# A GRU image scan on one core: the columns' second sum, t2, as a matmul with the unit matrix in 99 of 512 steps

## The reference, cut to what matters

```
def step(h, xg):
    hg = h @ W_hh.T + b_hh
    xr, xz, xn = jnp.split(xg, 3, axis=-1)
    hr, hz, hn = jnp.split(hg, 3, axis=-1)
    r = jax.nn.sigmoid(xr + hr)
    z = jax.nn.sigmoid(xz + hz)
    n = jnp.tanh(xn + r * hn)
    h_new = (1.0 - z) * n + z * h
    return (h_new, h_new)
...
return (right + down + left + up) / 4.0
```

## Time and profile before

| | |
|---|---|
| median of three runs | 2451.59 us |
| the profiled execution's own time | 2460.0 us |
| its span, first to last instruction | 2458.2 us |
| busy in the span: TensorE, VectorE, ScalarE, GpSimd | 88%, 81%, 65%, 62% |
| granted TensorE clock, mean over the span | 0.983 |

### The profile page before, as it was taken

The page is one execution under the profiler, slowest core; times in us unless marked ns, Lnnn a source line. Parts: engine busy times, 40 slices in busy tenths (PEclk is TensorE's granted clock), DMA queues, the critical chain, the costliest instruction groups (busy, mean ns, idle before and its releaser), DMA issues.

```text
span 2458.2 us, 81224 instructions
## 1 busy us (share of the span) xinstructions
PE 2158.5 (88%) x32176; PEld 1391.8 (57%) x32176; DVE 1997.6 (81%) x4912; ACT 1587.1 (65%) x3423; POOL 1534.5 (62%) x2119
## 2 busy tenths in 40 slices
PE   0679999899979999999979999999989999999993
PEld 0345555566646666566646666565646666665551
DVE  7309999877769999888869999888867887888883
ACT  0126666677757888677757788677757888887610
POOL 2007777667766777667766677667766777777710
PEclk9999999999989999999989999999999999999997
DMA  9993332245689998589999998589988666663379
GB/s 348 287 241 99 98 98 79 81 145 174 199 253 278 263 251 217 150 217 278 268 287 281 250 249 220 149 222 270 275 249 230 148 156 150 159 151 96 91 264 365
DMA packets 325720, 509.27 MB, mean 207 GB/s; under 512 B 24928, under 2 KB 140000, under 8 KB 325344
## 3 DMA queue, kind: packets, MB, share of 16 engines
q1 hardware_dynamic: 307296, 478.23, 70.0%
q10 hardware_dynamic: 18048, 25.85, 3.0%
HBM read 352.98 MB, written 151.01 MB: 205 GB/s over the span
## 4 chain that ended last, share of the span: by engine, by line
DVE 33%; PE 30%; ACT 17%; issue 7%; DMA 7%; POOL 3%; SPq 2%; ACTq 0%; DVEq 0%; POOLq 0%
PE bank L889 19%; DVE r L1033 11%; DVE r L1038 10%; ACT r L691 7%; DMA work<-x 5%; DVE h L1052 5%; ACT z L695 5%; DVE bank L1043 2%; ACT bank L699 2%; PE bank L869 2%; ACT work L686 2%; PE bank L871 2%; DVE bn L1025 2%; PE bank L890 1%; POOL hsum L567 1%
## 5 line engine op out<-in xcount | busy, mean ns | idle before, releaser
L889 PE MATMUL bank<-h,wh 64*64 64x256 f32 x6144 | 1493.4, 386 | 112.9 <-DVE h L1052 94.1
L869 PE MATMUL bank<-seq,wx 64*64 64x256 f32 x6144 | 1545.6, 384 | 31.3 <-DMA seq<-seq_next 22.6
L871 PE MATMUL bank<-seq,wx 64*64 64x256 f32 x6144 | 1547.4, 385 | 2.2 <-issue 2.2
L890 PE MATMUL bank<-h,wh 64*64 64x256 f32 x6144 | 1495.1, 387 | 0.0
L575 POOL TENSOR_TENSOR v<-z,h 128x256 f32<-128x256 f32 x1024 | 746.1, 729 | 617.8 <-ACT z L695 591.9
L889 PEld LDWEIGHTS bank<-h,wh 64*64 64x64 f32 x6144 | 713.1, 133 | 576.4 <-DVE h L1052 414.0
L869 PEld LDWEIGHTS bank<-seq,wx 64*64 64x64 f32 x6144 | 756.4, 133 | 194.4 <-DVE r L1038 94.4
L583 POOL TENSOR_TENSOR hsum<-hsum,h 128x256 f32<-128x256 f32 x1024 | 750.7, 733 | 129.3 <-DVE h L1052 106.9
L871 PEld LDWEIGHTS bank<-seq,wx 64*64 64x64 f32 x6144 | 754.5, 133 | 35.4 <-issue 4.2
L1033 DVE SCALAR_TENSOR_TENSOR r<-bank,bhh,r 128x256 f32<-128x256 f32 x1024 | 490.9, 479 | 277.3 <-ACT r L691 246.0
L890 PEld LDWEIGHTS bank<-h,wh 64*64 64x64 f32 x6144 | 704.1, 133 | 0.8
(11 more groups left out here) (94 smaller groups left out, 2441.4 us busy)
## 6 DMA issues: line engine op xcount, KB each, us to landing
work<-x SPq DMA_DIRECT2D x384, 384.0 KB, 6.2
work<-x SPq DMA_DIRECT2D x144, 512.0 KB, 6.0
out<-work SPq DMA_DIRECT2D x192, 384.0 KB, 4.9
work<-x SPq DMA_DIRECT2D x288, 128.0 KB, 6.0
work<-x SPq DMA_DIRECT2D x32, 768.0 KB, 6.5
seq_next<-work SPq DMA_DIRECT2D x48, 512.0 KB, 6.4
work<-hsum_last SPq DMA_DIRECT2D x48, 512.0 KB, 7.4
seq<-x SPq DMA_DIRECT2D x16, 512.0 KB, 7.0
```

The costliest lines, as they stand in the source:

```text
L869: pe.matmul(as_pair(ps[LOW, :], c), wx[HIGH, gate, :], px[HIGH], start=start, stop=False, skip_group_check=True)
L871: return pe.matmul(as_pair(ps[HIGH, :], c), wx[LOW, gate, :], px[LOW], start=start, stop=False, skip_group_check=True)
L889: pe.matmul(ps[LOW, 0:N2], wh[LOW, gate, :], state[LOW], start=start, stop=True, skip_group_check=True)
L890: return pe.matmul(ps[HIGH, 0:N2], wh[HIGH, gate, :], state[HIGH], start=start, stop=True, skip_group_check=True)
```

## The change

In the two stretches named above (the first pair's steps 0 to 69, and the fourth pair's steps 99 to 127: `t2_on_pe`), chain 1 is handled in another way:

- xn goes to bank 4 beside hn in place of bank 3; n and u go to the second half of bank 5, beside z, in place of bank 4.
- VectorE no longer makes t2 of chain 1. In its place TensorE multiplies t1 with the unit matrix and adds the product to xn in bank 4 (`add_t1`, two matmuls on the straight quarters), between x_n0 and x_z0. It waits for t1 and releases n.
- ScalarE's n of chain 1 reads bank 4 and writes bank 5; before, it read SBUF and wrote bank 4.
- x_z1 moves behind h_r1, and waits for h of chain 1. x_n1 now waits for n of the step before; x_r1 waits for r of the step before in place of t2.

```
+        def t2_on_pe(g, t):
+            return (g == 0 and t < PROJECT_FROM - 1) or (g + 1 == PAIRS and t > max(last_unit_at))
+        def xn_ps(g, t, c):
+            return hn_ps[1][:, N2:2 * N2] if c == 1 and t2_on_pe(g, t) else rx_ps[c][:, N2:2 * N2]
+        def n_ps(g, t, c):
+            return z_ps[1][:, N2:2 * N2] if c == 1 and t2_on_pe(g, t) else hn_ps[c][:, 0:N2]
+        def u_ps(g, t, c):
+            return z_ps[1][:, N2:2 * N2] if c == 1 and t2_on_pe(g, t) else hn_ps[c][:, N2:2 * N2]
...
-                act.activation(hn_ps[c][:, 0:N2], r[:, c, :], ACT.Tanh, bias=bih[:, 2:3]).then_inc(n_ready[c], 1)
+                before = xn_ps(g, t, c) if c == 1 and t2_on_pe(g, t) else r[:, c, :]
+                act.activation(n_ps(g, t, c), before, ACT.Tanh, bias=bih[:, 2:3]).then_inc(n_ready[c], 1)
...
+                if c == 1 and t > 0 and t2_on_pe(g, t - 1):
+                    pe.wait_ge(h_ready[1], state_before(g, t))
                 x_part(z_ps[c][:, 0:N2], 1, c, t, True).then_inc(x_z_ready[c], 1)
...
+                beside_state = c == 1 and t2_on_pe(g, t)
+                if beside_state and t > 0:
+                    if t2_on_pe(g, t - 1):
+                        pe.wait_ge(n_ready[1], T * g + t)
+                    else:
+                        pe.wait_ge(h_ready[1], state_before(g, t))
+                x_part(xn_ps(g, t, c), 2, c, t, beside_state).then_inc(x_rn_ready[c], 1)
...
+            def add_t1(g, t):
+                sums = xn_ps(g, t, 1)
+                pe.wait_ge(t1_ready[1], T * g + t + 1)
+                pe.matmul(sums[LOW], ident[LOW, :], r[LOW, 1, :], start=False, stop=True, skip_group_check=True)
+                pe.matmul(sums[HIGH], ident[HIGH, :], r[HIGH, 1, :], start=False, stop=True,
+                          skip_group_check=True).then_inc(t2_ready[1], 1)
...
-                    x_z(g, t, 1)
+                    if not t2_on_pe(g, t):
+                        x_z(g, t, 1)
 
                     h_r(g, t, 1)
+                    if t2_on_pe(g, t):
+                        x_z(g, t, 1)
...
+                    if t2_on_pe(g, t):
+                        add_t1(g, t)
                     if t + 1 < T:
                         x_z(g, t + 1, 0)
...
-                    make_t2(g, t, 1)
+                    if not t2_on_pe(g, t):
+                        make_t2(g, t, 1)
                     make_h(g, t, 0)
```

More of the change, by code:

```diff
@@ L880, in x_r @@
                 if T * g + t > 0:
-                    pe.wait_ge(t2_ready[c], T * g + t)
+                    pe.wait_ge(r_ready[1] if c == 1 and t > 0 and t2_on_pe(g, t - 1) else t2_ready[c], T * g + t)
                 x_part(rx_ps[c][:, 0:N2], 0, c, t, True)
             def x_n(g, t, c):
-                x_part(rx_ps[c][:, N2:2 * N2], 2, c, t, False).then_inc(x_rn_ready[c], 1)
+                beside_state = c == 1 and t2_on_pe(g, t)
[5 more added lines that the diff above has]
+                x_part(xn_ps(g, t, c), 2, c, t, beside_state).then_inc(x_rn_ready[c], 1)
             def h_part(ps, gate, t, c, start):
@@ L899, in h_n @@
             def h_n(g, t, c):
-                h_part(hn_ps[c], 2, t, c, True).then_inc(pre_n[c], 1)
+                h_part(hn_ps[c], 2, t, c, not (c == 1 and t2_on_pe(g, t))).then_inc(pre_n[c], 1)
+            def add_t1(g, t):
[4 more added lines that the diff above has]
+                          skip_group_check=True).then_inc(t2_ready[1], 1)
             def h_z(g, t, c):
@@ L1037, in make_t2 @@
                 dve.wait_ge(t1_ready[c], T * g + t + 1)
-                dve.tensor_tensor(r[:, c, :], rx_ps[c][:, N2:2 * N2], r[:, c, :], ALU.add).then_inc(t2_ready[c], 1)
+                dve.tensor_tensor(r[:, c, :], xn_ps(g, t, c), r[:, c, :], ALU.add).then_inc(t2_ready[c], 1)
             def make_u(g, t, c):
                 dve.wait_ge(n_ready[c], T * g + t + 1)
-                dve.scalar_tensor_tensor(out=hn_ps[c][:, N2:2 * N2], in0=z[:, c, :], scalar=1.0, in1=hn_ps[c][:, 0:N2],
+                dve.scalar_tensor_tensor(out=u_ps(g, t, c), in0=z[:, c, :], scalar=1.0, in1=n_ps(g, t, c),
                                          op0=ALU.subtract, op1=ALU.mult).then_inc(u_ready[c], 1)
@@ L1051, in make_h @@
                     dve.wait_ge(h_added[c], k - 1)
-                dve.tensor_tensor(h[:, c, t % 2, :], v[:, c, :], hn_ps[c][:, N2:2 * N2], ALU.subtract)\
+                dve.tensor_tensor(h[:, c, t % 2, :], v[:, c, :], u_ps(g, t, c), ALU.subtract)\
                    .then_inc(h_ready[c], 1)
```

## The result

The changed kernel takes 2446.32 us, median of 20 runs (2435.16 to 2450.19); the kernel before took 2455.64 on the same chip, median of 20 (2443.53 to 2466.44). The ratio is 0.9961 with a 95% interval of 0.9949 to 0.9973: 9.6 us faster, 6.6 to 12.5. The ratio is not the quotient of the two medians, and the medians can differ by a few us more or less; here they differ by 9.3 us. Two later measurements of the same program, beside the kernel before on two other occasions, gave 12.7 and 14.2 us (12.0 and 10.8 by the medians); all three, weighted by their intervals, give 11.2 us, with 2.3 either way. The forecast was a saving of 18.3 us.

What follows compares the result with a forecast made beforehand. A loop through several engines, with chain 1's t2 in it, was taken to bound the step; 13.0 us (first pair) plus 5.3 us (fourth) gave 18.3 us off 2451.59: 2433.3, say 2434 us, range 2429 to 2443.

Steps and rivals of the forecast that it cites:

- Loops A, B and C: Step loops: A through both chains without t2, 3.84 us; B chain 1's own, 3.85; C VectorE's order, first pair only, 3.85.
- Unknown (1): Link from t1 through TensorE's unit matmuls to n of chain 1: taken as 0.75 us, at best 0.69, at worst 1.18.
- Unknown (2): ScalarE's n of chain 1 from PSUM to PSUM: taken as 0.48 us, at most a tenth of a microsecond either way.
- The sum of 20.0 us by that rule: Whole saving if ScalarE's cheaper PSUM reads made n 43 ns shorter, leaving the 3.84 us loop to bind.
- Unknown (3): h_r1 on TensorE becoming a late starter: second pass 0.27 us behind the first, not 0.21, chain 1's loop then 3.90.
- rival 3: Unit matmuls take turns with x_z0 on TensorE: link 1.18 us, 24 us slower, 2475; chance 0.06.
- I put all of this at nothing: New waits of x_n1, x_r1 and x_z1 in TensorE's queue cost nothing; x_n1 has 0.06 us of room.
- Steps 64 to 69 ... I count them as the others: First pair's steps longer than 4.05 us, with u, t2, h in the same order, gain as much as plain steps.
- The fourth pair at 3.85 and 29 times 0.183: Fourth pair's 29 changed steps fall from 4.033 to 3.85 us each, saving 5.3 us.
- The other stretches step as before: Sign of being right: steps outside the two changed stretches keep their length.
- The end: Fourth pair's 5.3 us reach the program's end whole; the output stage begins and ends earlier by as much.
- rival 4: The program's end hides the fourth pair's saving: only 13.0 us remain, 2439; chance 0.25 together with another rival.

Runs made afterwards that it cites:

- no_t2: Kernel before with chain 1's t2 (and so xn in n) left out in the 99 steps, computing something else: 2438.14 us, ratio 0.9919.
- slow_first: Kernel before with one more VectorE operation between u of chain 0 and t2 of chain 1 in the first pair's steps 0 to 69: 2478.84 us, ratio 1.0091.
- long_link: Changed kernel with the two unit matmuls issued twice, the first time into a bank nobody reads: 2481.75 us, ratio 1.0088 against the kernel before.
- the six programs above: Six programs with TensorE code as before up to the fourth pair's changed steps; the steps the change leaves alone sum to 1289.3 us in their mean.
- slow_fourth: Kernel before with one more VectorE operation between u of chain 0 and t2 of chain 1 in the fourth pair's steps 99 to 127: 2463.4 us, ratio 1.0034.
- fourth_only: The change in the fourth pair's steps 99 to 127 alone, against the kernel before: 2452.81 us, ratio 0.9975.
- pad_after: Changed kernel with 158 small unneeded matmuls at the start of TensorE's program, against the kernel before: ratio 0.994, 14.7 us less.
- old_order: Changed kernel with x_z1 ahead of h_r1 again, keeping its new wait for h of chain 1: 2468.76 us in a single run, kernel before 2455.97.

## Why the prediction was right and where it was wrong

- **What bounds the step**: right. It is the loop h_r0, h_r1, r1, t1, u, h with t2 of chain 1 standing in it; without t2 the step is 3.850 (no_t2), with one more operation in that place it is longer by just that operation (slow_first).
- **Loops A, B and C at 3.84, 3.85, 3.85, taken as 3.86**: right, 3.863 measured (C not by itself, as said). Unknown (1), the link, is 0.75. Unknown (2): n from PSUM to PSUM is 0.45 us, 0.03 less than from SBUF. The rule of the Trainium skill (VectorE: DVE Perf Modes, section on the TRN2 errata) has 52 cycles for this difference, an estimate of 43 ns: the row goes the same way, with 0.03 of the 0.043 us. The sum of 20.0 us by that rule did not come. Unknown (3): the second pass of h_r1 starts 0.25 behind the first (378.91 and 379.16), 0.04 more than the 0.21 of an even beat. This and the shorter n about cancel.
- **x_r0 to x_z0 beside the unit matmuls**: right, so rival 3 is out; long_link, which makes the link 1.18 by force, shows the step that it would have given.
- **"I put all of this at nothing" for the waits**: right for the kernel as changed in the plain steps (h_r1 starts 1.35 us behind h_r0, 377.56 and 378.91, so x_n1's wait for n costs nothing). But I looked only at the waits in the new order and not at what that order is for. Left in front of h_r1, x_z1 would have cost 0.21 us a step.
- **"Steps 64 to 69 ... I count them as the others"**: wrong, though u, t2, h do stand in their loop. These six steps were 28.67 us before and are 29.23 after, with step 70 and 71 9.57 and 9.23: together 0.2 us more, where I had counted 1.1 less. That is 1.3 us of the 18.3. Steps 64 and 68 gained 0.17 and 0.20 us as forecast, and 69 and 70 together are as long as before (9.82 and 9.83). The rest lies in three steps. One is step 67, 5.10 where it was 4.64. The text ahead of the prediction says that TensorE has nothing but the scan's own work in steps 0 to 70. That is not so: behind x_z0 its queue has the matmuls of the group means in step 66 (L740, now L754) and those of the channel statistics in step 67 (L744 to L747, now L758 to L761), ahead of the next step's h_r0. VectorE and TensorE in step 67, before (t1 of chain 1, statistics, h of chain 0, h_r0):
```profile
454.07 0.48 DVE L1033 SCALAR_TENSOR_TENSOR r<-bank,bhh,r 128x256 f32<-128x256 f32 x1
...
454.74 0.38 PE L744 MATMUL bank<-mv,s_low 128*128 128x2 f32 x2
...
455.13 0.41 DVE L1052 TENSOR_TENSOR h<-v,bank 128x256 f32<-128x256 f32 x1
...
455.72 0.43 PE L889 MATMUL bank<-h,wh 64*64 64x256 f32 x1
```
  and after, with the unit matmuls (L928) ahead of them:
```profile
433.91 0.48 DVE L1068 SCALAR_TENSOR_TENSOR r<-bank,bhh,r 128x256 f32<-128x256 f32 x1
...
434.45 0.43 PE L928 MATMUL bank<-r,ident 64*64 64x256 f32 x1 [0.23 <-DVE r L1068]
...
435.05 0.38 PE L758 MATMUL bank<-mv,s_low 128*128 128x2 f32 x2
...
436.03 0.43 PE L911 MATMUL bank<-h,wh 64*64 64x256 f32 x1
```
  The unit matmuls wait for t1, which comes late in this step (its end is 2.76 us behind r0, in a plain step 2.32), and x_z0 and the statistics stand behind them in the queue: the statistics start 3.42 us behind the step's r0 where it was 2.95, and h_r0 starts 0.84 us behind the end of h (435.19) where it was 0.18. With the unit matmuls doubled (long_link) the step is 5.51, and without them (no_t2) 4.63. The other two are steps 65 and 66, 5.34 and 5.54 where they were 5.32 and 5.44. VectorE of the changed kernel, step 65:
```profile
420.44 0.43 DVE L1078 SCALAR_TENSOR_TENSOR bank<-z,bank 128x256 f32<-128x256 f32 x1 [0.44 <-ACT bank L713]
420.90 0.42 DVE L1087 TENSOR_TENSOR h<-v,bank 128x256 f32<-128x256 f32 x1
421.24 1.88 DVE L1143 BATCH_NORM_AGGREGATE mv<-bn 128x2 f32<-128x384 f32 x1
423.04 0.41 DVE L1068 SCALAR_TENSOR_TENSOR r<-bank,bhh,r 128x256 f32<-128x256 f32 x1
```
  An operation of 1.88 us stands between h of chain 1 and the next t1 of chain 0. From u to h of chain 0 it is 0.2 us less in step 65 too, but the long operation starts 0.49 us behind r0 (420.75) where it was 0.27, because h of chain 1 is that much later beside r0. The one takes back the other. That t2 of chain 1 still counted in step 65 is seen from no_t2 (4.97 us) and slow_first (5.65). In step 66 it did not count (5.49 in no_t2): there h_r0 (430.93) comes behind the matmuls of the group means (430.62 and 430.75), when h (ends at 430.54) is already there.
- **The fourth pair at 3.85 and 29 times 0.183**: 4.3 us in the trace, not 5.3. The step is 3.866 instead of 3.85 (0.4 us), and step 99, where the layouts change, took 4.43 us where it took 4.18 (0.2, and its own share of 0.2 not gained); the prediction left that wait out as small. The rest is the 29th step, whose end lies behind my count.
- **"The other stretches step as before"**: only nearly. The changed kernel's three traces have 2.6 us more in their mean than the six programs above, and more and longer pauses of TensorE; the measured times can't confirm it.
- **The end**: right. The effect of the fourth pair's steps reaches the end (slow_fourth 8.3 us for 9.2, fourth_only 6.1 for 4.0), so rival 4 is out. The output stage from the last r0 takes 112.3 to 116.6 us in all programs, 112.3 before and 113.7 after, without a pattern.

The failed step is the sum, "70 x (4.046 - 3.86) = 13.0 us, and 29 x (4.033 - 3.85) = 5.3 us: 18.3 us", in two of its assumptions. It multiplies by steps that do not have the forecast's last wait: steps 64 to 69, and step 99, whose wait was "left out". And it puts all else at nothing. From 18.3 it goes to 15.8 by the steps that gained less (0.2 of that is the 29th step, which the count leaves out), and to 13.2 with the pauses that the traces show. The three measurements together give 11.2, with 2.3 either way, which 13.2 fits; the first alone, 9.6 (6.6 to 12.5), lies just under it.

Whether the last 2 us are scatter or a cost stays open. There is one candidate that none of these terms holds, the start of the second pair's scan, beside full transfer queues. From r0 of step 127 of the first pair to r0 of step 14 of the second it is 81.7, 81.5 and 82.4 us in the changed kernel's three traces, with a pause of 2.3 to 3.1 us in each (2.84 us before 738.42 in the first). In the eight programs whose first pair is as before it is 76.6 to 81.7, 78.5 in the mean. But pad_after, with the same change, has 76.8, and no_t2 has 82.5 and yet measures 19.9 us less. So a cost there is not shown.

One more thing lay outside the mechanism: the forecast was taken off 2451.59, a median of three runs that lies 4 us below that of twenty. Off 2455.64 it would have been 2437, which the range holds, and the measured time would still have been 9 us above it.

Of the versions tried none is surely better than the change: pad_after's 14.7 us stand within the spread of the change's own three measurements.

## What to carry to other kernels

When one operation is taken out of a loop, work out every other loop through the same step, and multiply only by the steps whose last wait is that loop: steps with an operation of their own, as the aggregation here, steps in which the engine that gets the work has other work too, and the one where the layout changes are to be read one by one. When a matmul is added that waits, or an old one gets a new wait, ask what stands behind it in the queue (here the statistics' matmuls of step 67): put the consumer that needs the value first, and the one that only needs the bank behind it. And a forecast of half a per cent wants the median of many runs to start from: that of three lay 4 us off here.

## What I had not expected of the hardware

- A matmul that waits for a semaphore, placed ahead of one that waits for the same, delays the second one by 0.20 us (0.27 instead of 0.07 behind the end of h in old_order), although they run on different quarters of the array and start 0.12 us apart.
- TensorE has pauses of 0.3 to 3.1 us in the middle of its queue for which the profile names no cause. All 55 of them end 1.2 to 1.7 us behind a packet of 16384 bytes of the queue that carries its instructions. They come from 645 us on and sit at other places when code ahead of them gets longer.
- 48, 158 and 280 small matmuls at the start of the program all cost 5 us in the kernel before, with the granted clock at 0.61 instead of 1.00 in the stretch from 46 to 90 us (158 of them). In the changed kernel no such cost shows. 158 at the end, or 140 larger ones within the first scan, cost nothing that can be measured.
